# Cross-attention keys rotated, summed and cast on GpSimd instead of VectorE and ScalarE, and expert ids in 16 bits

## The reference

```
q = rotate(x Wq + bq)        keys = rotate(ctx Wk + bk)        v = ctx Wv + bv
rotate:  even' = even cos - odd sin,   odd' = even sin + odd cos
out = softmax(q keys^T / 8 + mask) v,  then Wo, bo and the residual
```

## Time and profile before

| | us |
|---|---|
| median of 3 runs | 2003.54 |
| lowest and highest | 2001.28, 2003.62 |
| profiled execution, its span from first to last instruction | 2002.3 |
| cross-attention, from its first to its last work | about 505 to 850 |
| routed experts, the loop | about 976 to 1440 |

### The profile page before, as it was taken

One profiled execution on the slowest core, in us unless ns is written; L12 is line 12 of the kernel. 1 busy time (PEld: TensorE's weight loads), 2 busy tenths in 40 slices (PEclk: granted clock), 3 DMA queues, 4 the chain that ended last, 5 costly groups with the idle time before them and its releaser, 6 DMA issues. The chain is left out here.

```text
span 2002.3 us, 33243 instructions
## 1 busy us (share of the span) xinstructions
PE 1765.5 (88%) x11070; PEld 1108.0 (55%) x11070; DVE 1442.3 (72%) x2729; ACT 1052.5 (53%) x2220; POOL 993.1 (50%) x740
## 2 busy tenths in 40 slices
PE   7957887889889999898799999997899989998799
PEld 4433444444567676644444444444744746665699
DVE  6768999995578888758676766664754367886893
ACT  4776667672588887734665655664322231114342
POOL 1269889892462222004577777775000028664342
PEclk9979999999899999999899999998989989999799
DMA  2033443332576656240166665734830053435540
GB/s 72 0 124 110 138 138 127 121 129 80 120 170 157 160 142 161 68 142 24 44 217 213 204 194 169 238 96 130 265 99 1 17 168 116 136 123 179 197 133 17
DMA packets 138159, 257.43 MB, mean 129 GB/s; under 512 B 30661, under 2 KB 94822, under 8 KB 135318
## 3 DMA queue, kind: packets, MB, share of 16 engines
q1 hardware_dynamic: 120358, 212.16, 35.5%
q0 software_dynamic: 13824, 37.77, 6.2%
q10 hardware_dynamic: 3808, 5.38, 1.1%
HBM read 205.82 MB, written 49.44 MB: 127 GB/s over the span
## 5 line engine op out<-in xcount | busy, mean ns | idle before, releaser
L2355 POOL TENSOR_TENSOR soft_power<-soft_logit,soft_high 128x1024 f32<-128x1024 f32 x28 | 66.2, 2363 | 290.8 <-DVE soft_high L2429 290.5
L3211 PE MATMUL moe_up_ps<-moe_w_tile,ahead 128*64 128x352 f32 x1152 | 193.5, 480 | 0.9 <-issue 0.7
L3148 POOL DMA_INDIRECT moe_y<-ahead,moe_where x144 | 157.3, 1092 | 64.4 <-issue 38.7
L3355 ACT ACTIVATE moe_w_tile<-moe_w 128x1216 f32 x144 | 175.1, 1217 | 20.5 <-issue 19.0
L1791 ACT ACTIVATE xattn_prob<-xattn_sm,xattn_least 112x375 f32<-112x375 f32 x256 | 155.0, 606 | 53.5 <-DVE xattn_least L1692 48.7
L1692 DVE CUSTOM_DVE_ANT_0 xattn_sm<-xattn_s_ps,wide 112x375 f32<-112x375 f32 x256 | 137.7, 542 | 53.3 <-PE xattn_s_ps L1574 30.3
L3142 POOL DMA_INDIRECT ahead<-moe_tok,moe_where x144 | 147.4, 1024 | 57.0 <-issue 42.1
L1584 PE MATMUL xattn_pt_ps<-ident,xattn_prob 112*125 112x112 f32 x768 | 131.3, 280 | 24.0 <-ACT xattn_pt L1797 13.5
L1584 PEld LDWEIGHTS xattn_pt_ps<-ident,xattn_prob 112*125 112x125 f32 x768 | 112.9, 190 | 63.9 <-ACT xattn_prob L1791 43.2
L1023 POOL TENSOR_TENSOR mamba_x_state<-mamba_x_state,mamba_cx_all 128x896 f32<-128x896 f32 x64 | 133.7, 2088 | 26.0 <-DVE mamba_x_state L1081 25.9
L1017 POOL TENSOR_TENSOR xn<-mamba_u,mamba_b_all 128x896 f32<-128x896 f32 x64 | 133.6, 2090 | 14.9 <-DMA mamba_b_all<-mamba_b 14.9
(11 more groups left out here) (454 smaller groups left out, 4279.6 us busy)
## 6 DMA issues: line engine op xcount, KB each, us to landing
moe_w<-moe_w SPq DMA_DIRECT2D x64, 480.0 KB, 3.8
soft_w<-soft_w SPq DMA_DIRECT2D x16, 1024.0 KB, 7.1
mamba_b_all<-mamba_b SPq DMA_DIRECT2D x32, 448.0 KB
mamba_cx_all<-mamba_c SPq DMA_DIRECT2D x32, 448.0 KB, 3.8
mamba_cy_all<-mamba_c SPq DMA_DIRECT2D x32, 448.0 KB, 4.7
moe_w_tile<-moe_y SPq DMA_DIRECT2D x14, 1024.0 KB, 7.6
soft_logits<-soft_logit SPq DMA_DIRECT2D x28, 512.0 KB, 2.6
soft_logit<-soft_logits SPq DMA_DIRECT2D x14, 1024.0 KB, 5.1
```

The lines of the kernel that those rows point to most:

```text
L3148: pool.indirect_dma_start(y_dram, bass.IndirectOffsetOnAxis(ap=where[:, 1, t:t + 1], axis=0), y_sb[:, 2 * s + i], None).then_inc(y_stored[ ...
L3211: mm = pe.matmul(up_ps[n * HALF:(n + 1) * HALF, i, 0:2 * I], xT[:, s % 2, at:at + HALF], w_tile[:, s, i, n, h * 2 * I:(h + 1) * 2 * I], st ...
L3355: place_weights = weight_placer(act, 0, lambda to, src: act.activation(to, src, ACT.Copy))
```

## The change

In the cross-attention, ScalarE copies the projected keys from PSUM into `key` and adds the bias (`keep_keys`, at h = 3 and 6; the second copy gives `k_read`). GpSimd makes the four products from there (`turn_keys`), then the sums as before, and the three casts (`cast_keys`), each right behind the work that it depends on. VectorE rotates no keys and ScalarE casts none. The order of the other work on each queue stays. At the start of the stage the same is done for the keys of batch 1. In the routed experts the ids of the experts are held as unsigned 16-bit numbers in SBUF and DRAM.

```diff
+U16 = mybir.dt.uint16
...
-            KEYS_AT, ROTATE_AT, CAST_AT = (0, 1, 2, 4), (2, 3, 5, 6), (8, 12, 15)
+            KEYS_AT, KEEP_KEYS_AT = (0, 1, 2, 4), (3, 6)
...
             def _(pool):
+                def turn_keys(b):
+                    pool.wait_ge(k_read, b + 1)
+                    for n, table in enumerate((k_cos, k_sin, k_sin, k_cos)):
+                        last = pool.tensor_tensor(turn[:, n], key[:, n // 2], table, ALU.mult)
+                    last.then_inc(k_turned, 1)
+
                 def sum_keys(b):
-                    pool.wait_ge(k_read, b + 1)
-
-                    wait(pool, k_cast, PARTS * b)
+                    pool.wait_ge(k_turned, b)
                     pool.tensor_tensor(key[:, 0], turn[:, 0], turn[:, 2], ALU.subtract)
                     pool.tensor_tensor(key[:, 1], turn[:, 1], turn[:, 3], ALU.add).then_inc(k_whole, 1)
...
+
+                def cast_keys(b, n):
+
+                    if n == 0:
+                        pool.wait_ge(k_whole, b + 1)
+                    else:
+                        pool.wait_ge(k_less, (PARTS - 1) * b + n)
+
+                    wait(pool, k_stored[n], 16 * b)
+                    pool.tensor_copy(part[:, n], key[:]).then_inc(k_cast, 1)
...
                 pool.memset(v[:], 0.0).then_inc(v_cleared, 1)
+                turn_keys(1)
                 sum_keys(1)
+                cast_keys(1, 0)
                 pool.wait_ge(q_whole, 2)
                 for n in range(PARTS - 1):
                     lessen_keys(1, n)
+                    cast_keys(1, n + 1)
                     lessen_queries(OTHERS, n)
                 for b in range(B - 2):
                     if b < NCH - 1:
                         turn_queries(OTHERS + 1 + b)
+                    turn_keys(b + 2)
                     sum_keys(b + 2)
+                    cast_keys(b + 2, 0)
                     for n in range(PARTS - 1):
                         if b < NCH - 1:
                             lessen_queries(OTHERS + 1 + b, n)
                         lessen_keys(b + 2, n)
+                        cast_keys(b + 2, n + 1)
...
-                def rotate_keys(b, n):
-                    m = n // 2
-                    if n == 0:
-
-                        wait(dve, k_whole, b)
-                    if n % 2 == 0:
-                        dve.wait_ge(kproj_ready, DH * b + m + 1)
-                    table = (k_cos, k_sin, k_sin, k_cos)[n]
-                    product = dve.scalar_tensor_tensor(turn[:, n], kv_ps[:, m, 0:S2], bk[:, m:m + 1], table, ALU.add, ALU.mult)
-                    if n == 3:
-                        product.then_inc(k_read, 1)
...
-                        if follows(b, 2) and h in ROTATE_AT:
-                            rotate_keys(b + 2, ROTATE_AT.index(h))
...
-                for n in range(2):
-                    rotate_keys(1, n)
                 lessen_first(0)
-                for n in range(2, 4):
-                    rotate_keys(1, n)
                 lessen_first(1)
...
-                def cast_keys(b, n):
-                    if n == 0:
-                        act.wait_ge(k_whole, b + 1)
-                    else:
-                        act.wait_ge(k_less, (PARTS - 1) * b + n)
-
-                    wait(act, k_stored[n], 16 * b)
-                    act.activation(part[:, n], key[:], ACT.Copy).then_inc(k_cast, 1)
+                def keep_keys(b, m):
+                    if m == 0:
+
+                        act.wait_ge(k_cast, PARTS * b)
+                    act.wait_ge(kproj_ready, DH * b + m + 1)
+                    kept = act.activation(key[:, m], kv_ps[:, m, 0:S2], ACT.Identity, bias=bk[:, m:m + 1])
+                    if m == DH - 1:
+                        kept.then_inc(k_read, 1)
...
-                        if follows(b, 2) and h in CAST_AT:
-                            cast_keys(b + 2, CAST_AT.index(h))
+                        if follows(b, 2) and h in KEEP_KEYS_AT:
+                            keep_keys(b + 2, KEEP_KEYS_AT.index(h))
                         if follows(b) and h in COPY_VALUES_AT:
                             copy_values(b + 1, 1 - s, COPY_VALUES_AT.index(h))
 
-                for n in range(PARTS):
-                    cast_first(n)
+                cast_first(0)
+                for m in range(DH):
+                    keep_keys(1, m)
+                cast_first(1)
+                cast_first(2)
                 keep_queries(2)
...
-                cast_keys(1, 1)
                 cast_queries(OTHERS, 1)
                 copy_values(0, 0, 2)
                 keep_queries(4)
-                cast_keys(1, 2)
                 cast_queries(OTHERS, 2)
...
-    expert_dram = k.dram("moe_expert", [HR * P], I32)
+    expert_dram = k.dram("moe_expert", [HR * P], U16)
...
-        expert_row = k.sb(ctx, "moe_expert_row", [1, HR * P], I32)
...
-            expert = sb("expert", [P, HR], I32)
+            expert = sb("expert", [P, HR], U16)
```

More of the change, by code:

```diff
@@ L1309, in cross_attention @@
         q_kept, q_turned = k.sem("xattn_q_kept"), k.sem("xattn_q_turned")
+        k_turned = k.sem("xattn_k_turned")
         kproj_ready, k_read, k_whole = first_keys.ready, first_keys.read, first_keys.whole
@@ L1852, in batch @@
                             store_sums(b - 1, 1 - s)
-                        if follows(b, 2) and h in CAST_AT:
-                            cast_keys(b + 2, CAST_AT.index(h))
+                        if follows(b, 2) and h in KEEP_KEYS_AT:
+                            keep_keys(b + 2, KEEP_KEYS_AT.index(h))
                         if follows(b) and h in COPY_VALUES_AT:
                             copy_values(b + 1, 1 - s, COPY_VALUES_AT.index(h))
-                for n in range(PARTS):
-                    cast_first(n)
+                cast_first(0)
[3 more added lines that the diff above has]
+                cast_first(2)
                 keep_queries(2)
-                cast_keys(1, 0)
                 cast_queries(OTHERS, 0)
@@ L2693, in routed_experts @@
         w = k.sb(ctx, "moe_w", [P, RING, WN])
-        expert_row = k.sb(ctx, "moe_expert_row", [1, HR * P], I32)
+        expert_row = k.sb(ctx, "moe_expert_row", [1, HR * P], U16)
         ends_row = k.sb(ctx, "moe_ends_row", [1, E], I32)
```

## The result

The changed kernel takes 2066.73 us (median of 4 runs, 2061.57 to 2069.85), the kernel before 2002.41 on the same chip in turn: a ratio of 1.032, with a 95% interval of 1.0296 to 1.0343. The forecast was 2009.5 with a range up to 2017. It had the sign right and a tenth of the size. The profiled execution took 2061.57 us, with a span of 2059.7. It is the shortest of the four; the other three took 4 to 8 us more, at a mean granted clock of 0.952 to 0.956 against its 0.959.

What follows compares the result with a forecast made beforehand. TensorE, busy 88% of the span, was taken as the bound. Steady batches -1, batches 0 to 2 with the start +7.0 and ids 0 summed to +6.0 us: 2008.3, plus 1.2 to the median, 2009.5; range 1998 to 2017.

Steps and rivals of the forecast that it cites:

- Batches 0 to 2: Cross-attention while queries are prepared: GpSimd's longer queue delays ScalarE's query casts, each batch 2.8 us longer, 8.4 us.
- The chain from the keys read to the second subtraction: GpSimd's queue in batches 0 to 2, products to second lessened query: 12.5 us against ScalarE's 9.7 us.
- the clock term: Cost of a lower TensorE clock behind stalls in batches 0 to 2; the forecast's sum holds none.
- rival 3: Much slower: GpSimd dearer, +10 to +14 us, and TensorE's clock lower behind stalls, 1 us each fall; 2018; chance 0.11.
- the wait at h = 6: Steady batches: TensorE's value projections wait for ScalarE's second key copy and start 0.7 us late.
- Steady batches: Cross-attention batches 3 to 13: -0.1 us per batch for 11 batches, -1 us; bounds -13 to +4 us.
- what pays for it: Steady batches: ScalarE's three dropped 0.82 us casts and TensorE's vanished small late starts make up the 0.7 us by h = 12.
- Rival 1: Faster: the context load is not last in most batches, so each steady batch gains 1.1 us; 1997.5 us; chance 0.17.
- Start: Start of the cross-attention stage: one key cast leaves ScalarE's queue ahead of the first exp, -0.7 us.
- a load free or twice as long: Experts' register loads: taken as unchanged, 0 us; bounds of 1.1 us per load, 18 times, giving -4 to +4 us.
- a fifth at most as reaching TensorE: Experts' loop: at most a fifth of any changed register-load time reaches TensorE, as ScalarE's loads lie in slack.
- Rival 4: Routed experts: the narrower ids matter, 4 us either way; chance 0.03.

Runs made afterwards that it cites:

- copy_at_5: The change's cross-attention part with 32-bit ids (AND with 63 ahead of the weight wait), second raw key copy at head 5 instead of 6; ratio 1.0104 to the kernel before.
- order_alone: The change's cross-attention part with 32-bit ids, GpSimd's two query subtractions put ahead of key sums in batches 0 to 2; ratio 1.0068 to the kernel before.
- casts_moved: The kernel before with only the three key casts a batch moved from ScalarE to GpSimd, VectorE still rotating keys; ratio 1.0065 to the kernel before.

## Why the prediction was wrong

**The sign and the mechanisms of cross-attention were right, the sizes were not.** *Batches 0 to 2*: forecast +8.4, measured +16.4, and +4.1 more in batch 3. The chain from the keys read to the second subtraction was forecast at 12.5 us and takes 566.85 to 579.4, 12.5 us. The idle time that came of it is less than forecast: TensorE's waits behind ScalarE's exps and copies of weights grow by 3.5 us in the three batches, not 8.4. (The added idle time above is made of these and 2.8 us of waits for the key copy, less 1.2 us of waits that went.) The failed step is the clock term: the forecast puts it at nothing, and rival 3, which has it, at "1 us for each fall". The clock fell in each of the three batches and stayed at the lower level for some two fifths of each (a mean of 0.81 between 0.5 and 1): 11.6 us, 3.9 a batch. Rival 3 had the right mechanism at a quarter of its price. What makes it so dear is the two kinds of wait together: TensorE's busy time in these batches is 11.6 us over before with both, 4.8 in copy_at_5, which has the stalls without the wait at h = 6, and 1.1 in order_alone, which has that wait and stalls of 1.9 us. The text also counted one fall of the clock in the stage before; there is a second, at the start of batch 0 (0.96 over that batch).

*Steady batches*: the wait at h = 6 was forecast at 0.7 and measured 0.71. The step that failed is "what pays for it ... at h = 12 both kernels are level". The engines' waits behind a late start are links of one chain from scores to exp to transposes, and move with it. Forecast -0.1 a batch, measured +1.0 to 1.1; copy_at_5 gives 0.9 of it back. Rival 1 (faster) had nothing to stand on for the same reason: TensorE is busy 18.5 of 19.8 us, and what is left belongs to the chain and the context load, not to ScalarE's amount of work: casts_moved took 2.0 us a batch from it and gained nothing.

*Start*: forecast -0.7; from the first key projection to that of batch 0 it takes 25.14 us after, 24.92 before. In the six other kernels that copy and cast as the change does it is 24.5 to 24.7, so 0.2 to 0.4 us of the gain is there; in the profiled run of the change the clock was at the lower level for longer in this stretch.

*Prices*: the cast on GpSimd, forecast 1.0 with bounds 0.65 and 1.6, is 0.81 us. A product there, forecast 0.85, is 0.92 to 0.95. The copy on ScalarE, forecast 0.53, is 0.56. The Trainium skill ("GPSIMD Engine Reference", section 3.1) gives 1.96 times VectorE's time for a two-input operation. Here the product's 0.95 us against VectorE's 0.60 is 1.6, though VectorE's instruction is another one, which reads PSUM and adds the bias as well.

**The ids were the large miss.** The text had "the register loads stay 18 on each of two engines, 1.02 and 1.10 us". Their number stays, their price is 3.5 times as high. The bound, a load free or twice as long, rested on no row: every load of ids in the trace was of 32-bit neighbours. The second half failed too, "a fifth at most as reaching TensorE" and the slack on ScalarE: of 2.6 us more a load 1.8 reached the time (31.1 us over 17 intervals), and either engine alone did it. A total of waits of 100.5 us in 70 places says nothing of the place where a load stands, ahead of the first placing copy of its group. Rival 4 named the part and gave it 3% and 4 us.

The Trainium skill ("Runtime: NRT & Kernel Launch", section "Instruction fetch mechanics") gives a register load as about 200 ns a register even in bulk, for loads from HBM that the runtime issues. The row of ids lies in SBUF, so it is not the same load; here elements of 16 bits or with gaps come near that figure (0.23 us), and neighbouring 32-bit words do not (0.06 us).

## What to carry to other kernels

Ahead of a register load look at the form of what it reads: 32-bit neighbours were four times cheaper an element than the two other forms tried, 16-bit elements and words with a gap, and narrower values should be packed and read as words. Work moved to an engine with time to spare is judged by what it stands in front of in that engine's queue, first of all where another engine is served from the same queue; the cheapest repair can be the order, as long as the engine still gets through its work in time. And where TensorE is the bound, price each new stall with the clock it may lose behind it, not with its own length, and look for a second, short wait beside it: here the two together cost far more clock than the stall alone.

## What the runs showed of the hardware

- A register load of 16 neighbouring 32-bit words takes 1.02 us on ScalarE and 1.10 on VectorE, of 8 words 0.55 and 0.60; of 16 elements that are 16-bit, or 32-bit with a gap, 3.6 and 3.8.
- In the kernel after, TensorE's stalls of 1.8 to 2.6 us for ScalarE were each followed by a granted clock of half for several us, and so was the wait of 0.7 us in the middle of batches 1 to 3: busy time of the same matmuls 23.3 us a batch at a mean of 0.81, 18.5 at 1.00. With both in each batch the clock cost 11.6 us in three batches, more than twice the 4.8 us of added idle time; with stalls of 2.6 us alone 4.8 us; with the short wait and stalls of 1.9 us 1.1 us, as of the three stalls only one was followed by the lower clock.
- GpSimd was busy for 98% of a batch (21.63 of 21.98 us) in an order that serves ScalarE first, and ScalarE's query casts waited 0.3 us for it. When the batches became as short as its work, it fell behind, and a stall of 2.6 us came back in the third batch.
